# The split of the mixed rounds and the normalisation on ScalarE, the first layer's one-hot on ScalarE in three parts

## What is computed

```python
def layer(x, src, dst, attr, ...):
    xj0, xj1 = split(x[dst])                      # 64 scalars, 32 x 3 vectors
    m0, m1 = products_with(attr) + linear(xj0, xj1)
    agg = segment_sum(merge(m0, m1), src, N)      # sum of the edges of a node
    a0, a1 = split(agg); x0, x1 = split(x)
    u0 = einsum('nu,nv,uvw->nw', x0, a0, Wss) * c + einsum('nui,nvi,uvw->nw', x1, a1, Wvv) * c
    u1 = einsum('nu,nvi,uvw->nwi', x0, a1, Wsv) * c + einsum('nui,nv,uvw->nwi', x1, a0, Wvs) * c
    return x + merge(u0 + x0 @ L0 * c, u1 + linear(x1, L1) * c)
x = layernorm(x + layer0(x)); x = layernorm(x + layer1(x))
```

## Time and profile before

| | |
|---|---|
| Time, median of 3 runs | 9364.85 us (9337.15 to 9369.23) |
| The profiled execution's own time | 9380.0 us |
| Its span in the trace | 9378.3 us |
| Busy: PE, VectorE (DVE), ScalarE (ACT), GpSimd (POOL) | 6593.8, 6945.2, 2700.6, 4379.0 us |
| First sweep | about 3010 to 6700 us |
| Second sweep | about 6800 us to the end |
| Mean granted TensorE clock | 0.837 |

### The profile page before, as it was taken

How to read it: one execution, slowest core, us unless ns; L and a number is a source line. 1 busy time by engine, 2 the same in 40 slices (tenths; PEclk the granted TensorE clock), 3 DMA queues, 4 the chain that set the end, 5 groups by cost and what they waited for, 6 DMA issues and landing times.

```text
span 9378.3 us, 137567 instructions
## 1 busy us (share of the span) xinstructions
PE 6593.8 (70%) x37295; PEld 4930.3 (53%) x37295; DVE 6945.2 (74%) x8811; ACT 2700.6 (29%) x9170; POOL 4379.0 (47%) x3378
## 2 busy tenths in 40 slices
PE   3555555545554887788777887888678888888887
PEld 2443444434443655565556555656455566555665
DVE  4555555555555977777777777777489999999999
ACT  1222222222221222222222222222234444444443
POOL 1555555555555366556665666566622222222221
PEclk6777777767777988888888888888799999999999
DMA  5666565656653455555555555555321111211121
GB/s 176 197 185 187 184 185 185 197 176 187 194 185 109 141 180 177 176 184 180 177 175 184 180 178 176 183 180 180 124 77 68 66 66 66 71 66 66 66 72 46
DMA packets 692541, 1372.63 MB, mean 146 GB/s; under 512 B 106047, under 2 KB 500077, under 8 KB 666863
## 3 DMA queue, kind: packets, MB, share of 16 engines
q10 hardware_dynamic: 84636, 590.82, 20.1%
q1 hardware_dynamic: 455091, 499.42, 17.6%
q0 software_dynamic: 152736, 281.45, 9.0%
HBM read 587.20 MB, written 784.08 MB: 146 GB/s over the span
## 4 chain that ended last, share of the span: by engine, by line
PE 40%; issue 25%; DVE 18%; another core or an unknown queue 11%; ACT 3%; ACTq 1%; SPq 1%; DMA 1%; DVEq 1%; POOL 0%; POOLq 0%
PE node_ps L1169 9%; PE prods_ps L1138 7%; PE turn_ps L1158 7%; DVE work L930 6%; PE m_ps L1073 4%; DVE upd L936 3%; DVE work L917 2%; PE node_ps L1073 2%; PE node_ps L1181 2%; DVE upd L921 2%; PE s_ps L1073 2%; PE s_ps L1055 2%; PE turn_ps L1024 1%; PE prods_ps L1043 1%
## 5 line engine op out<-in xcount | busy, mean ns | idle before, releaser
L578 POOL DMA_INDIRECT slots<-pay,slot x3136 | 3259.9, 1040 | 1880.3 <-issue 1535.5
L635 POOL TENSOR_TENSOR q<-xt,yv 125x3072 f32<-125x3072 f32 x200 | 1095.6, 5478 | 3050.5 <-PE turn_ps L1158 3021.1
L1169 PE MATMUL node_ps<-msgs,onehot 128*125 128x160 f32 x6800 | 1289.6, 342 | 683.8 <-issue 665.7
L930 DVE TENSOR_TENSOR work<-prods_ps,yv 125x1024 f32<-125x1024 f32 x1200 | 1392.3, 1215 | 455.3 <-remote 439.3
L1169 PEld LDWEIGHTS node_ps<-msgs,onehot 128*125 128x125 f32 x6800 | 1154.3, 219 | 921.3 <-issue 921.1
L1139 PE MATMUL prods_ps<-w_bil,ys_t 64*125 64x512 f32 x2400 | 1372.5, 668 | 2.1 <-issue 2.1
L936 DVE TENSOR_REDUCE upd<-work 125x48 f32<-125x3072 f32 x400 | 1341.2, 3353 | 13.7
L1158 PEld LDWEIGHTS turn_ps<-ident,q 125*128 125x128 f32 x9600 | 1137.0, 196 | 181.4 <-issue 175.7
L1158 PE MATMUL turn_ps<-ident,q 125*128 125x125 f32 x9600 | 1185.9, 281 | 3.7 <-ACT q_t L1405 3.4
L1138 PE MATMUL prods_ps<-w_bil,a_t 64*125 64x512 f32 x1600 | 890.4, 660 | 325.9 <-DVE work L917 238.2
L917 DVE TENSOR_TENSOR work<-prods_ps,xt 125x1024 f32<-125x1024 f32 x800 | 956.8, 1217 | 71.2 <-issue 44.8
(11 more groups left out here) (220 smaller groups left out, 9298.1 us busy)
## 6 DMA issues: line engine op xcount, KB each, us to landing
msgs<-slots ACTq DMA_DIRECT2D x200, 1428.0 KB, 6.2
slots<-zero ACTq DMA_DIRECT2D x183, 1386.0 KB
win<-table SPq DMA_DIRECT2D x784, 160.0 KB
picks<-pick_b SPq DMA_DIRECT2D x196, 512.0 KB
pick_b<-picks SPq DMA_DIRECT2D x196, 512.0 KB
table<-tab SPq DMA_DIRECT2D x200, 350.0 KB
slots<-pay,slot POOLq DMA_INDIRECT x3136
spill_in<-spill_sums SPq DMA_DIRECT2D x200, 80.0 KB, 2.0
```

The lines of the kernel that those rows point to most:

```text
L578: g.indirect_dma_start(out=slots[layer][:, :], out_offset=bass.IndirectOffsetOnAxis(ap=slot[q][:, j:j + 1], axis=0), in_=pay[q][:, j, :], ...
L635: g.tensor_tensor(q3[0:HM, :].rearrange("p (i u v) -> p i u v", i=3, u=V), xt[nb][0:HM, S:D].rearrange("p (u i) -> p i u", i=3).unsqueeze( ...
L930: ve.tensor_tensor(wk[:, i, :, :].rearrange("p w (h k) -> p h w k", h=2), prods_ps[r % 2][0:HM, :].rearrange("p (h w k) -> p h w k", h=2, ...
L1169: te.matmul(node_ps[0:HM, 0:D], onehot[:, j, :], msgs[b][:, j, 0:D], start=(j == 0), stop=False)
```

## The change

In layer 1, GpSimd does the multiplications of components 1 and 2 of the mixed rounds. It can't read PSUM, so ScalarE copies each mixed round to SBUF first (`prods_out`), between its other copies; VectorE keeps component 0 (`DIRECT`), both multiplications ahead of both sums. GpSimd's q of tile t moves from step t + 1 to the end of step t (`outer(1, k)`), and GpSimd adds q's three components itself, so that PE turns 4 blocks with 4 transposes in place of 12 matmuls. In both layers `linear` begins with a matmul of x with twice the identity and the weights give the features in the order of h, so h is one addition (in layer 1 out of PSUM); the mean, the centred values, the deviation and the scaling by its inverse run on ScalarE, and only the reciprocal stays on VectorE, now behind the third of its multiplications. In layer 0 the one-hot moves to ScalarE, as distances and selections in three parts (`HOT`) at three places of the step.

```diff
+HOT = (0, 4, 11, BLOCKS)
+DIRECT = (3, 1)
+USES = [R0 + d * R1 for d in DIRECT]
+        mixed_work = [picks[:, 0:3 * ROUND], work[:, 0:3 * ROUND]]
+        prods_sb = [pay[q].rearrange("p j f -> p (j f)")[:, 0:ROUND] for q in range(2)]
...
 # GpSimd, layer 1
+                        for j in range(R1):
+                            g.wait_ge(s["copied"], R1 * n + j + 1)
+                            if j == 1:
+                                g.wait_ge(s["upd"], RS_ALL * n + R0)
...
+                            for i in range(DIRECT[1], 3):
+                                mul = g.tensor_tensor(wk[:, i], prods_sb[j][0:HM, :].rearrange("p (h w k) -> p h w k", h=2, k=V),
...
+                            mul.then_inc(s["mixed_mul"], 1)
+                    if within(t, 0, NT):
+                        outer(1, k)
+                        n = t
+                        for j in range(2):
+                            g.wait_ge(*((s["q_part"], 2 * n + 1) if j else (s["q_mul"], n + 1)))
+                            add = g.tensor_tensor(q3[0:HM, 0:VV], q3[0:HM, 0:VV], q3[0:HM, VV * (j + 1):VV * (j + 2)], ALU.add)
+                            add.then_inc(s["q_part"], 1)
...
 # VectorE
-                ve.tensor_tensor(onehot[:, :, :], msgs[b][:, :, LOCAL:LOCAL + 1].broadcast_to([P, BLOCKS, HM]),
-                                 node_iota[:, :].unsqueeze(1).broadcast_to([P, BLOCKS, HM]), ALU.is_equal).then_inc(s["hot"], 1)
...
+                        if r == 2 and within(t, 2, NT + 1):
+                            inverse(layer, t - 2)
...
-                if within(t, 2, NT + 2):
-                    normalise(layer, (t - 2, half - 1, b))
...
-                    for i in range(3):
+                    if layer == 1:
+                        ve.wait_ge(s["copied"], R1 * n + r - R0 + 1)
+                    for i in range(DIRECT[layer]):
...
-                    mixed(R0)
+                    for r, part in ((R0, mixed_mul), (R0, mixed_sum), (R0 + 1, mixed_mul), (R0 + 1, mixed_sum)) if layer == 0 else (
+                            (R0, mixed_mul), (R0 + 1, mixed_mul)):
+                        part(r)
                 if nodes:
-                    mixed(R0 + 1)
-                    ve.wait_ge(s["lin_out"], 2 * n + 2)
+                    if layer == 1:
+                        mixed_sum(R0)
+                    if layer == 1:
+                        mixed_sum(R0 + 1)
...
-                    ve.scalar_tensor_tensor(h[0:HM, :], X, 2.0, lin[0:HM, :], ALU.mult, ALU.add).then_inc(s["h_part"], 1)
...
-                    ve.tensor_tensor(h[0:HM, :], h[0:HM, :], upd[0:HM, :], ALU.add).then_inc(s["h_part"], 1)
...
-                    ve.tensor_reduce(stats[0:HM, 0:1], h[0:HM, :], AX_X, ALU.add).then_inc(s["h_part"], 1)
...
-                    ve.tensor_scalar(stats[0:HM, 1:2], stats[0:HM, 0:1], -1.0 / D, None, ALU.mult).then_inc(s["h_ready"], 1)
...
+                    ve.tensor_tensor(h[0:HM, :], lin[0:HM, :] if layer == 0 else node_ps[0:HM, 0:D], upd[0:HM, :], ALU.add).then_inc(s["h_ready"], 1)
+
+            def inverse(layer, n):
+                s = LS[layer]
+                ve.wait_ge(s["deviation"], 4 * n + 4)
+                ve.reciprocal(stats[0:HM, 4:5], stats[0:HM, 3:4]).then_inc(s["inverse"], 1)
...
 # PE
+                        if layer == 1:
+                            mm = te.transpose(turn_ps[:, HM * j:HM * j + HM], q3[0:HM, o:o + P], idn)
+                            continue
...
-                    te.matmul(node_ps[0:HM, S:D], v_t[:, :], w.lin1[:, :], start=True, stop=True)
-                    te.matmul(node_ps[0:HM, 0:S], ys_t[:, :], w.lin0[:, :], start=True, stop=False)
+                    te.matmul(node_ps[0:HM, 0:D], ident2[0:HM, 0:HM], xt[nb][0:HM, :], start=True, stop=False)
+                    te.matmul(node_ps[0:HM, S:D], v_t[:, :], w.lin_u[:, :], start=False, stop=False)
+                    te.matmul(node_ps[0:HM, 0:S], ys_t[:, :], w.lin0[:, :], start=False, stop=False)
...
 # ScalarE
+                ac.activation(sq[0:HM, :], h[0:HM, :], ACT.Identity, scale=-1.0 / D, accum_out=stats[0:HM, 1:2]).then_inc(s["deviation"], 1)
+                ac.wait_ge(s["deviation"], 4 * n + 1)
+                ac.activation(centred[0:HM, :], h[0:HM, :], ACT.Identity, bias=stats[0:HM, 1:2]).then_inc(s["deviation"], 1)
+                ac.wait_ge(s["deviation"], 4 * n + 2)
+                ac.activation(sq[0:HM, :], centred[0:HM, :], ACT.Square, accum_out=stats[0:HM, 2:3]).then_inc(s["deviation"], 1)
...
+                ac.activation(res[b][0:HM, :], centred[0:HM, :], ACT.Copy, scale=stats[0:HM, 4:5]).then_inc(s["normed"], 1)
...
+                def prods_out(j):
...
+                    ac.copy(prods_sb[j][0:HM, :], prods_ps[(R0 + j) % 2][0:HM, :]).then_inc(s["copied"], 1)
...
                 if within(t, 2, NT + 2):
                     deviation(layer, t - 2)
+                if layer == 0 and edges:
+                    selections(0, 3 * t + 2, HOT[1], HOT[2])
                 paid(0, 2)
                 paid(0, 3)
+                if within(t, 2, NT + 2):
+                    normalise(layer, (t - 2, half - 1, b))
+                if layer == 0 and edges:
+                    distances(0, k, HOT[2], HOT[3])
                 features()
+                if layer == 0 and edges:
+                    selections(0, 3 * t + 3, HOT[2], HOT[3]).then_inc(s["hot"], 1)
+                prods_out(0)
                 turned_q(0)
+                prods_out(1)
                 where(1)
                 summed()
...
+                if layer == 0 and within(t, 0, NT - 1):
+                    distances(0, later(k), HOT[0], HOT[1])
                 turned_q(1)
                 paid(1, 0)
                 linear_out()
                 turned_y()
+                if layer == 0 and within(t, 0, NT - 1):
+                    selections(0, 3 * t + 4, HOT[0], HOT[1])
                 paid(1, 1)
...
                 paid(1, 3)
+                if layer == 0 and within(t, 0, NT - 1):
+                    distances(0, later(k), HOT[1], HOT[2])
```

More of the change, by code:

```diff
@@ L143, in build @@
         ident = sb("ident", [P, P])
+        ident2 = sb("ident2", [P, P])
         after = sb("after", [P, P])
@@ L900, in node_step @@
                 n, nb, nh = t - 1, 1 - b, half if b == 1 else half - 1
+                if not nodes and within(t, 2, NT + 2):
+                    inverse(layer, t - 2)
                 if nodes:
@@ L1472, in one_hot, with selections @@
                     ac.wait_ge(s["edges_done"], t)
-                for j in range(BLOCKS):
+                for j in range(j0, j1):
                     last = ac.activation(onehot[:, j, :], node_iota[:, :], ACT.Square, bias=msgs[b][:, j, LOCAL:LOCAL + 1], scale=-1.0)
-                last.then_inc(squared, 1)
-                ac.wait_ge(squared, t + 1)
-                ac.activation(onehot[:, :, :], onehot[:, :, :], ACT.Relu, bias=ones_f[:, 0:1], scale=-2.0).then_inc(s["hot"], 1)
+                last.then_inc(squared[layer], 1)
+            def selections(layer, times, j0, j1):
+                ac.wait_ge(squared[layer], times)
+                return ac.activation(onehot[:, j0:j1, :], onehot[:, j0:j1, :], ACT.Relu, bias=ones_f[:, 0:1], scale=-2.0)
+            def one_hot(k):
+                distances(1, k, 0, BLOCKS)
+                selections(1, k[0] + 1, 0, BLOCKS).then_inc(LS[1]["hot"], 1)
             def first_msgs(layer):
```

162 lines of the change are left out of this document (92 added, 70 removed).

## The result

The changed kernel took 9306.7 us (median of 6 runs, 9292.5 to 9328.4), the kernel before 9362.0 us beside it: a ratio of 0.995 (95% interval 0.9935 to 0.9965). The profiled run is 9304.8 us long, 73.5 us less than before. The forecast for this run was 9222 us, 158 us less, about twice that gain; as a median it was 9207 us, again 158 us less, where the medians differ by 55.

A forecast was written before the change was run, and what follows sets the result against it. VectorE bounds the second sweep; a loop of GpSimd, standstill and PE bounds the first. 9380 - 130 (second sweep) - 18 (first) - 10 (steps without scatters) = 9222 us profiled, 9207 us as median; range 8990 to 9400.

The forecast's parts named there:

- the penalty of 1.65: Second sweep: after some 4 us idle, PE's clock is halved for 3.3 us, making the loop 1.65 us longer.
- The check of the branch: Second sweep: ScalarE's new copies, GpSimd's multiplications and VectorE's last sum stay off the 22.3 us loop, with room.
- my third of a longer operation: Second sweep: a 1024-element GpSimd operation takes a third of L635's 5.47 us, 1.82 us.
- its h and normalisation go at nothing: First sweep: VectorE's busy time isn't on the loop, so moving its h and normalisation changes nothing.
- 37.3 - 1.9 + 1.7 = 37.1: First sweep: a step's gain and loss from moving the one-hot nearly cancel; -18 us over 92 steps.
- The 1.9: First sweep: without VectorE's one-hot beside the second indirect DMA, GpSimd and the standstill's end come 1.91 us earlier.
- The 1.7: First sweep: the late one-hot on ScalarE puts 12 records of sum_edges behind the standstill, costing 1.7 us a step.
- (2): First sweep: standstill's end doesn't follow GpSimd, or the page's rule holds; +156 us, median 9381, no change; 14%.
- (1): Second sweep: VectorE sets the step at 18.9 us; -640 us, median 8700; 5%.
- (3): Second sweep: all PE work of the loop at half clock, step 32.0 us; +670 us, median near 10,005; 9%.
- (4): Second sweep: GpSimd over 3.1 us an operation; at 4 us, step 29.5 us, +420 us, median near 9756; 4%.
- (5): First sweep: the standstill shrinks or goes without VectorE's one-hot; up to -2 us more a step, 9020; 4%.

The follow-up runs named there:

- e4: Changed kernel with the second layer's reciprocal behind VectorE's fourth multiplication and third sum instead of behind the third multiplication: 9282 us, ratio 0.993.
- e2: Kernel before with only the first layer's one-hot moved to ScalarE in three parts: 9318 us, ratio 0.996.
- e1: Changed kernel with the first layer's one-hot back on VectorE behind h: 9362 us, ratio 1.000.
- e3: Changed kernel with ScalarE's four payload copies of a chunk's first half ahead of the deviation and the one-hot's middle Relu: 9289 us, ratio 0.993.
- e10: Changed kernel with the last Relu of the first layer's one-hot ahead of ScalarE's features, slower surroundings: 9132 us, ratio 0.978.
- e5: Changed kernel with the first layer's mean, reciprocal and scaling back on VectorE and its deviation in two instructions, quicker surroundings: 8047 us, ratio 1.045.
- e6: e5 without the first layer's matmul of x, with the second layer's reciprocal late and ScalarE's first copy ahead, quicker surroundings: 7674 us, ratio 0.996.
- e9: Changed kernel, unchanged, run again in slower surroundings: 9120 us, ratio 0.978 against the kernel before there.
- e16: Changed kernel with the last Relu of the first layer's one-hot ahead of ScalarE's features, quicker surroundings: 7550 us, ratio 0.980.
- e8: Kernel before, unchanged, run again in slower surroundings: 9333 us.
- e17: Kernel before, unchanged, in quicker surroundings: 7697 us.
- e15: Changed kernel, unchanged, in quicker surroundings: 7910 us, ratio 1.026.

## Why the prediction was right and wrong

**The second sweep: right, in size and in mechanism.** -139.8 us against -130. The terms, forecast in brackets: one-hot to deviation 7.05 (7.05), deviation to reciprocal 1.7 (1.8), round 5 2.0 (1.1) and `sum_edges` 5.5 (5.0), both in part at half clock, which I had put into the penalty of 1.65; step 23.9 (24.0). The check of the branch held as well: VectorE's last sum was to end 23 us behind the one-hot and its third multiplication to come at 29, where "the loop wants that only at 31"; they are at 24.0 and 28.9, and VectorE then waits 2.6 us. One row of it was wrong and cost nothing: GpSimd's last multiplication was to end at 18.6, 0.9 us ahead of the sum that needs it. At 2.36 us an operation it ends at 20.5, and the sum waits 1.3 us. The error came behind the prediction, in e4's expectation, which didn't work out what the moved reciprocal puts into the branch. The estimate from the GPSIMD Engine Reference of the Trainium skill (3.1, Elementwise), 2.25 us, was nearer to the 2.36 of the trace than my third of a longer operation, 1.82.

**The first sweep: the step that failed is "its h and normalisation go at nothing".** -18 us were forecast and +94.0 measured. The prediction put the normalisation, h and the matmul of x at nothing, as VectorE isn't on the loop and ScalarE's added instructions "lie in its idle time". In the first surroundings they cost 1.7 us a step (the changed kernel's 38.6 against the 36.9 of e2, which has the one-hot's move alone) and 1.8 (e1's 39.3, which has them without the one-hot, against 37.5). Over 92 steps that is some 160 us; the one-hot's 0.6 takes off 55. I had written that each microsecond lost on the payload copies would be 92; they were held not by ScalarE's added work (e3), but by the standstill itself. Counting ScalarE idle by its busy share was no argument there.

**The sum for the one-hot, "37.3 - 1.9 + 1.7 = 37.1", had nearly the right size and the wrong mechanism.** -0.2 was forecast, -0.6 measured (e2). The 1.9: the indirect DMAs did lose their stretch, 0.96 for 2.87 with the one-hot off VectorE. The Trainium skill's page SBUF — State Buffer (Who interferes with whom) has it that a tensor_tensor doesn't stall the making of descriptors; the trace disagrees again. But I let the standstill's end move with GpSimd and its beginning stay. In fact the beginning moved from q + 21 to q + 14; it cut off the last payload copies, GpSimd's last DMA came 1.4 us later instead of 1.9 earlier, and the end moved by 0.2. The 1.7: hot isn't on the path with slow transfers (e10), yet all of `sum_edges` did come behind the standstill, for another reason (PE was held up at rounds 4 and 5).

**Which part of the rest?** Which of normalisation, h and the matmul of x costs the 1.7 us, no run shows: e5 and e6, made for that, fell to quick transfers. And e9 shows the whole change at 37.0, with round 5 where e2 has it, in other surroundings of nearly the same speed; there the rest seems to cost nothing. That 37.0 is the 37.1 of the forecast by luck, as neither term of the sum came out. What decides between 37.0 and 38.6, and the mechanism of the standstill, stay open. That it is absent in the surroundings with quick transfers is shown; that it is a backlog of transfers is only argued, and it may as well be what makes the transfers slow.

**The rivals.** (2), the 1.7 lost without the 1.9, is nearest in size for the first sweep (+156 against +94) and was given 14%, but not in mechanism: the one-hot's move gains (e2). (1), (3) and (4) didn't come: the step wasn't 19 us, PE wasn't at half clock throughout, GpSimd was under 3.1 us. (5), a shorter standstill, gives a gain of the size that e9 has, but nothing shows its mechanism. Not among them was what quick transfers bring: there the change costs 2.6%, as the late hot puts `sum_edges` behind the load of x, and what VectorE gains counts for nothing with PE full (e16). That mechanism was in the prediction, at 1.7 us; where nothing hides it, it is 4.1, of which over 1 is PE's lower clock behind the wait.

**The small terms.** The eight steps without scatters gave -5.4 (forecast -10). The -12.1 us ahead of the sweeps were forecast as none; between e8 and e9 that part moved by -2.2 us, between e17 and e15 by +3.1, so I count it as chance.

## What to carry to other kernels

Before a wait is moved out of a loop, work out what the move puts into the branches that had room: e4 cut one loop of 23.9 us and made another, of at most 21.3, as long, and gained nothing. Work that is added to an idle engine isn't free for that; give it a term, and a run that has it alone. When a stretch in which everything stands still moves, ask where it will now begin, and what will then be behind it, not only where it will end. A mean step can hide a spread of 5 us: look at single steps before two means are compared. Don't put work behind a load that it doesn't need (hot behind `features`): it costs nothing until something else gets faster.

## What the runs showed of the hardware

The same kernel took 9362 and 7702 us, at 187 and 257 GB/s in the stretch 1000 to 2000 us, with the DMA engines as long busy for a byte, and the sign of the change's effect turned with it: 0.995 and 0.978 against 1.026. In the slower surroundings, while the later of the sixteen indirect DMAs run, signals between engines come late (VectorE waited 9.6 us for one, which came 1.5 us behind the twelfth DMA) and PE begins records of `sum_edges` 0.7 to 2.8 us apart; in the quicker ones the same DMAs at the same pace bring nothing of the kind. A VectorE operation of 128x2125 on two inputs in SBUF stretched the indirect DMA beside it from 0.96 to 2.87 us. PE ran at a granted clock of 0.50 behind 3.3 us of idle time. A GpSimd operation on two inputs in SBUF of 1024 elements takes 2.36 us, 2.31 ns an element, one of 3072 with both inputs broadcast 5.47 us, 1.78 ns an element.
